# A gated-scan plus ternary-FFN layer on eight cores: layer-norm output transposed on TensorE instead of by DMA, absolute sums moved from VectorE to ScalarE

## The chip, the cores and the metric

The kernel runs on all 8 cores of one Trainium2 chip. Every core executes the same program on its own two sequences (4096 tokens of 2048 channels); the cores exchange nothing. The metric is the device time in microseconds of the slowest core.

## What is computed

The reference, cut to what matters. Every core holds x as [4096, 2048], T=2048 tokens in a sequence, C=2048, H=5120.

```python
x = x + layernorm(attn(layernorm(x), W, b))
x = x + layernorm(ffn(layernorm(x), w_fc, w_proj))

def attn(x, W, b):                       # W: [2C, C]
    gates, values = split(x @ W.T + b)
    gates, values = sigmoid(gates), tanh(values)
    return scan(h[t] = gates[t] * h[t-1] + values[t])

def ternarize(w):
    abs_mean = max(mean(abs(w)), 1e-5)
    thr = 0.7 * abs_mean                 # +1 / -1 / 0, times abs_mean
...
def ffn(x, w_fc, w_proj):
    h = square(relu(x @ ternarize(w_fc).T))
    return h @ ternarize(w_proj).T
```

## The kernel before

The program is a sequence of three stages, each with its own buffers; the five engines (TensorE, VectorE, ScalarE, GpSimd, SyncE) run instruction lists of their own that meet in semaphores.

*Stage 1* (lines 194 to 448) is the one the change touches. GpSimd first casts W to bf16 in HBM and SyncE loads it transposed (`wt_sb`, lines 223 to 226). Then the tokens are worked off in 16 chunks k of 256 tokens (NCH=16, CH1=256). For one chunk: SyncE loads x (`x_sb`, line 234, one buffer); VectorE takes mean and variance (`stats_seg`, lines 46 to 268); ScalarE takes the square root (line 366) and writes the normalised bf16 rows `xnb_sb` (line 371, `ln1_seg`); ScalarE stores them to HBM (`xn_s`, line 377), and SyncE reads them back with 16 transposing DMAs into `xnT_sb` (line 239, three buffers), channels on partitions. TensorE multiplies 32 output groups of 128 channels, a gate group and a value group for each of the 16 channel pairs, each group 16 matmuls of 128x256 (line 418), into four PSUM buffers `ps_par`. ScalarE takes sigmoid and tanh out of PSUM (`evac_seg`, lines 388 and 394), VectorE runs the scan along the tokens for each pair (`scan_seg`, line 285) and keeps its last column in `carry` (line 291). GpSimd stores the 16 pairs of the chunk at once (`h_t`, line 448). `h_sb` has one buffer: the first scan of a chunk waits until the store of the chunk before has landed.

Beside that, stage 1 sums the absolute values of both FFN weight matrices, which gives the two thresholds. The matrices are cut into 320 pieces of 128x512 f32, 20 for each chunk (`wave(k)`). GpSimd loads them into `wslab`, a ring of four buffers (line 445; piece ip waits until piece ip-4 has been summed, semaphore `v_abs`), and VectorE reduces each (`abs_seg`, line 301).

The order of work is written out by hand. On VectorE it is stats of chunk k, scans of chunk k-1, the 20 absolute sums of wave k, then stats of k+1. On ScalarE it is `ln1_seg(k)`, then the 32 evacuations of chunk k-1. On GpSimd it is the 20 loads of wave k, then a wait for all scans of chunk k, then the store of `h_t`. TensorE runs ahead of ScalarE by up to four groups, the depth of `ps_par`:

```python
_w(tensor, s_ev4, gi - 3)      # group gi waits for the evacuation of gi-4
```

After the last chunk VectorE and TensorE exchange a few tiny operations that turn the sums into thresholds (lines 321 to 355, semaphore `fz`).

*Stage 2* (from line 503) reads `h_t` back, transposes it on TensorE (line 573), adds the layer norm of the scan to x, and makes and transposes the ternary weights (lines 583, 551). Its first load, `htin_sb`, waits for every `h_t` store. *Stage 3* (from line 748) is the FFN: matmuls at lines 921 and 933, the long TensorE-bound part. Neither is changed.

Of the kernel before, what the change touches and what calls it, by code (L numbers as in the profile page):

```python
# [53 lines left out]
def build_program(cfg):  # L54
# [47 lines left out]
    with est:  # L102
# [25 lines left out]
        d_xnT4 = ring("d_xnT4", 3); p_mm4 = sem("p_mm4"); s_ev4 = sem("s_ev4")  # L128
        v_sc4 = sem("v_sc4"); v_cr4 = sem("v_cr4"); d_hw4 = ring("d_hw4")
# [48 lines left out]
        with nc.Block() as block:  # L178
# [17 lines left out]
            with contextlib.ExitStack() as sp1:  # L196
# [4 lines left out]
                xnT_sb = sb1("xnT_sb", [128, 3, NC, CH1], BF16)  # L201
# [11 lines left out]
                acc_pj = sb1("acc_pj", [128, NPJP], F32)  # L213
                ps_par = [sp1.enter_context(nc.psum_tensor(f"ps_par{i}", [128, 512], F32))
                          for i in range(4)]
                ps_misc = sp1.enter_context(nc.psum_tensor("ps_misc", [128, 512], F32))
                GP1 = 2 * NG

# [11 lines left out]
                @block.sync  # L230
                def _(sync):
                    for k in range(NCH):
                        _w(sync, s_nm4, TT1 * k)
                        rinc(sync.dma_start(out=x_sb[:, 0, :, :],
                                       in_=x_ch1[k]), d_x4, k)
                        rwait(sync, d_xnw4, k)
                        _w(sync, p_mm4, GP1 * (k - 2))
                        for ct in range(NC):
                            sync.dma_start(
                                out=xnT_sb[:, k % 3, ct, :],  # L240
                                in_=xn_d[k * CH1:(k + 1) * CH1, ct * 128:(ct + 1) * 128],
                                transpose=True).then_inc(d_xnT4[k % 3], 16)
# [3 lines left out]
                def _(vector):  # L246
# [28 lines left out]
                    def scan_seg(vector, k):  # L275
                        for pair in range(NG):
                            gp = k * NG + pair
                            vector.wait_ge(s_ev4, k * GP1 + 2 * pair + 2)
                            rwait(vector, d_hw4, k - 1)
                            if k % RESET == 0:  # L280
                                init = 0.0
                            else:
                                vector.wait_ge(v_cr4, (k - 1) * NG + pair + 1)
                                init = carry[:, pair:pair + 1]
                            vector.tensor_tensor_scan(  # L285
                                out=h_sb[:, 0, pair, :],
                                data0=g_sb[:, gp % 2, :], data1=v_sb[:, gp % 2, :],
                                initial=init, op0=ALU.mult,
                                op1=ALU.add).then_inc(v_sc4, 1)
# [5 lines left out]
                    def abs_seg(vector, k):  # L295
                        for ip in wave(k):
                            rwait(vector, d_wf, ip)
                            kind, a, b, w = pieces[ip]
                            dst = (acc_fc[:, ip:ip + 1] if kind == "fc"
                                   else acc_pj[:, ip - NFCP:ip - NFCP + 1])  # L300
                            vector.tensor_reduce(
                                out=dst, in_=wslab[:, ip % 4, 0:w], axis=AX.X,
                                op=ALU.add, apply_absolute_value=True).then_inc(v_abs, 1)
# [57 lines left out]
                def _(scalar):  # L361
                    scalar.wait_ge(d_prep, 48)

                    def ln1_seg(scalar, k):
# [4 lines left out]
                        rwait(scalar, d_xnw4, k - 1)  # L369
                        for tt in range(TT1):  # L370
# [30 lines left out]
                    for k in range(1, NCH):  # L401
                        ln1_seg(scalar, k)
                        evac_seg(scalar, k - 1)
                    evac_seg(scalar, NCH - 1)

                @block.tensor
                def _(tensor):
                    tensor.wait_ge(d_wt3, 32 * NC)
                    for k in range(NCH):
                        tensor.wait_ge(d_xnT4[k % 3], 16 * NC * (k // 3 + 1))  # L410
                        for pair in range(NG):
                            for role in range(2):
# [4 lines left out]
                                for ct in range(NC):  # L417
# [3 lines left out]
                                        xnT_sb[:, k % 3, ct, :],  # L421
# [550 lines left out]
```

## Time and profile before

| | us |
|---|---|
| five timed runs | 6057.26, 6140.46, 5746.21, 5724.54, 6313.94 |
| their median | 6057.26 |
| the profiled execution | 5741.26 |
| its span, slowest core (core 1) | 5739.7 |
| spans of the other cores | 5702.9 to 5739.6 |

Stage 1 fills the span from its start to about 1907 us, stage 2 to about 2900 us, stage 3 the rest. Times within the trace are microseconds from the start of the span of core 1. In rows of a timeline the first number is the start, the second the time that the row covers; x4 means four instructions merged; the brackets give the idle time of the engine before the row and what ended it.

### The profile page before, as it was taken

What the parts mean: (1) busy time and instruction counts of PE and PEld (TensorE: products, weight loads), DVE (VectorE), ACT (ScalarE), POOL (GpSimd) and SP (SyncE); (2) the same over time, 40 slices, a digit from 0 to 9 for tenths busy, and PEclk for the clock granted to TensorE, in tenths of its full rate; (3) what the DMA queues carried; (4) which work ended last, traced back from release to release, by engine and by line L of the source; (5) the groups of instructions that cost most, each with busy time, mean ns of one, the idle gap of its engine ahead of it and who ended that gap; (6) DMA issues with size and microseconds to landing.
All of it is one profiled execution on the core that took longest, in us unless ns stands there. A gap on an engine that the chain in (4) does not pass through costs nothing.

```text
span 5739.7 us, 60974 instructions; the slowest of 8 cores (5702.9 to 5739.7 us)
## 1 busy us (share of the span) xinstructions
PE 3700.8 (64%) x20742; PEld 2163.6 (38%) x20742; DVE 1492.1 (26%) x2686; ACT 1227.9 (21%) x2768; POOL 246.5 (4%) x460
## 2 busy tenths in 40 slices
PE   0056647466465444443439799596996969879697
PEld 0045536455464322222214344243443434434343
DVE  0022333333333366666610200202002020020101
ACT  0012222121221223232322030220302213031120
POOL 0000110101101000000000000000000000000000
PEclk9977878778787655555569899798997979989898
DMA  9843333433333577776576574655646556474553
GB/s 110 173 114 103 115 115 102 132 104 114 116 101 118 176 245 249 249 243 237 191 185 154 168 174 157 184 156 177 169 143 190 153 189 155 149 191 154 161 151 135
DMA packets 1007452, 918.51 MB, mean 160 GB/s; under 512 B 887216, under 2 KB 887344, under 8 KB 956976
## 3 DMA queue, kind: packets, MB, share of 16 engines
q1 hardware_dynamic: 900528, 486.74, 30.7%
q0 software_dynamic: 47232, 276.85, 16.5%
q10 hardware_dynamic: 59392, 151.02, 8.3%
q8 instruction: 176, 2.88, 0.2%
q14 instruction: 124, 1.02, 0.1%
HBM read 704.76 MB, written 192.94 MB: 156 GB/s over the span
## 4 chain that ended last, share of the span: by engine, by line
PE 58%; DMA 13%; DVE 10%; issue 6%; ACT 5%; SPq 3%; another core or an unknown queue 3%; ACTq 1%; DVEq 0%; POOL 0%; POOLq 0%
PE ps_pj L933 19%; PE ps_fc L921 19%; PE ps_par L418 14%; DMA x_sb<-x 4%; DMA wslab<-wpj 3%; DMA wslab<-wfc 3%; PE ps_bf L583 3%; DVE st6c L46 2%; PE ps_yT L944 2%; DMA sfc_sb<-sfcT_t 2%; ACT stage_fc L551 1%; ACT stage_pj L551 1%; DVE st6a L46 1%; DVE out_sb L811 1%
## 5 line engine op out<-in xcount | busy, mean ns | idle before, releaser
L418 PE MATMUL ps_par<-xnT_sb,wt_sb 128*128 128x256 bf16 x8192 | 948.1, 281 | 957.4 <-ACT g_sb L388 656.0
L921 PE MATMUL ps_fc<-xn1T_sb,sfc_sb 128*128 128x512 bf16 x5120 | 1134.8, 385 | 290.0 <-DMA sfc_sb<-sfcT_t 248.2
L418 PEld LDWEIGHTS ps_par<-xnT_sb,wt_sb 128*128 128x128 bf16 x8192 | 825.5, 101 | 1079.7 <-issue 961.5
L933 PE MATMUL ps_pj<-hfc_sb,spj_sb 128*128 128x512 bf16 x5120 | 1106.5, 379 | 15.6 <-ACT hfc_sb L852 15.6
L921 PEld LDWEIGHTS ps_fc<-xn1T_sb,sfc_sb 128*128 128x128 bf16 x5120 | 506.4, 99 | 916.6 <-issue 331.7
L933 PEld LDWEIGHTS ps_pj<-hfc_sb,spj_sb 128*128 128x128 bf16 x5120 | 500.3, 98 | 621.7 <-issue 19.9
L46 DVE BATCH_NORM_STATS2 st6c<-ps_yT 128x6 f32<-128x512 f32 x128 | 79.7, 684 | 2367.2 <-PE ps_yT L944 2367.2
L583 PE MATMUL ps_bf<-idbf_sb,ssl 128*128 128x128 bf16 x1280 | 295.8, 265 | 357.3 <-DVE ssl L657 160.2
L848 ACT ACTIVATE r_sb<-ps_fc,am_fc 128x512 f32<-128x512 f32 x320 | 220.0, 687 | 686.8 <-PE ps_fc L921 682.8
L583 PEld LDWEIGHTS ps_bf<-idbf_sb,ssl 128*128 128x128 bf16 x1280 | 134.2, 105 | 521.7 <-issue 484.8
L285 DVE TENSOR_TENSOR_SCAN h_sb<-g_sb,carry,v_sb 128x256 f32<-128x256 f32 x224 | 168.1, 750 | 602.5 <-ACT v_sb L394 593.2
L860 ACT COPY y_sb<-ps_pj 128x512 f32<-128x512 f32 x128 | 75.0, 586 | 1039.6 <-PE ps_pj L933 1039.6
L573 PE MATMUL ps_hT<-id_sb,htin_sb 128*128 128x128 f32 x512 | 115.2, 419 | 193.7 <-DVE x1o_sb L629 180.8
L944 PE MATMUL ps_yT<-id_sb,y_sb 128*128 128x128 f32 x512 | 100.8, 380 | 207.2 <-DVE out_sb L811 207.2
L852 ACT ACTIVATE hfc_sb<-r_sb 128x512 bf16<-128x512 f32 x320 | 201.3, 629 | 30.0 <-ACT r_sb L848 0.7
L366 ACT ACT_TABLE_LOAD x15 | 19.2, 1283 | 853.7 <-DVE veps L257 853.7
L388 ACT ACTIVATE g_sb<-ps_par,bT_sb 128x256 f32<-128x256 f32 x256 | 121.4, 474 | 343.4 <-PE ps_par L418 312.5
L394 ACT ACTIVATE v_sb<-ps_par,bT_sb 128x256 f32<-128x256 f32 x256 | 121.5, 475 | 299.2 <-PE ps_par L418 299.2
L551 ACT COPY stage_fc<-ps_bf 128x128 bf16<-128x128 bf16 x640 | 146.0, 266 | 178.2 <-PE ps_bf L583 160.5
L551 ACT COPY stage_pj<-ps_bf 128x128 bf16<-128x128 bf16 x640 | 151.8, 266 | 144.9 <-PE ps_bf L583 121.9
L573 PEld LDWEIGHTS ps_hT<-id_sb,htin_sb 128*128 128x128 f32 x512 | 104.3, 226 | 201.1 <-issue 199.2
L944 PEld LDWEIGHTS ps_yT<-id_sb,y_sb 128*128 128x128 f32 x512 | 92.0, 201 | 216.2 <-issue 214.5
(75 smaller groups left out, 1676.6 us busy)
## 6 DMA issues: line engine op xcount, KB each, us to landing
sfc_sb<-sfcT_t SPq DMA_DIRECT2D x320, 512.0 KB, 4.9
spj_sb<-spjT_t SPq DMA_DIRECT2D x128, 1280.0 KB, 6.2
wslab<-wfc POOLq DMA_DIRECT2D x160, 256.0 KB, 4.2
wslab<-wpj POOLq DMA_DIRECT2D x160, 256.0 KB, 3.6
wslab<-wfc ACTq DMA_DIRECT2D x160, 256.0 KB, 4.9
wslab<-wpj ACTq DMA_DIRECT2D x160, 256.0 KB, 4.0
x_sb<-x SPq DMA_DIRECT2D x16, 2048.0 KB, 8.5
h_t<-h_sb POOLq DMA_DIRECT2D x16, 2048.0 KB, 9.5
```

What stands on the lines that cost most here:

```text
L46: ins = vec.bn_stats(st6[:, 6 * j:6 * j + 6], src[:, j * step:(j + 1) * step])
L285: vector.tensor_tensor_scan(out=h_sb[:, 0, pair, :], data0=g_sb[:, gp % 2, :], data1=v_sb[:, gp % 2, :], initial=init, op0=ALU.mult, op1=A ...
L394: scalar.activation(out=v_sb[:, gp % 2, :], in_=ps_par[gi % 4][:, 0:CH1], func=AF.Tanh, bias=bT_sb[:, NG + pair:NG + pair + 1]).then_inc(s ...
L418: ins = tensor.matmul(pp[:, 0:CH1], wt_sb[:, ct, col0:col0 + 128], xnT_sb[:, k % 3, ct, :], start=(ct == 0), stop=(ct == NC - 1))
L551: scalar.copy(out=dst, in_=ps_bf[t % 2][0:128, 0:128]).then_inc(s_ev2, 1)
L573: tensor.transpose(ps_hT[hf][:, ctl * 128:(ctl + 1) * 128], htin_sb[:, k % 2, ct, tt * 128:(tt + 1) * 128], id32[:, :]).then_inc(p_tr7, 1)
L583: tensor.transpose(ps_bf[t % 2][0:128, 0:128], ssl2[:, ip % 2, ctl * 128:(ctl + 1) * 128], idbf[:, :]).then_inc(p_tr2, 1)
L848: scalar.activation(out=r_sb[:, 0, :], in_=ps_fc[gh % 2][:, 0:CH2], func=AF.Relu, scale=am_fc[:, 0:1]).then_inc(s_rev, 1)
L852: scalar.activation(out=hfc_sb[:, ht, :], in_=r_sb[:, 0, :], func=AF.Square).then_inc(s_sqq, 1)
L921: ins = tensor.matmul(ps_fc[gh % 2][:, 0:CH2], sfc_sb[:, gh % 3, ct, :], xn1T_sb[:, q % 2, ct, :], start=(ct == 0), stop=(ct == NC - 1))
L933: ins = tensor.matmul(ps_pj[gc % 2][:, 0:CH2], spj_sb[:, gc % 2, ht, :], hfc_sb[:, ht, :], start=(ht == 0), stop=(ht == NH - 1))
L944: tensor.transpose(ps_yT[:, ct * 128:(ct + 1) * 128], y_sb[:, ct, tt * 128:(tt + 1) * 128], id32[:, :]).then_inc(p_yt, 1)
```

## The change

The layer-norm output no longer goes through HBM. After ScalarE has written `xnb_sb`, TensorE transposes it in 128x128 blocks into two new PSUM tiles `ps_xt` (`xt_group`, four groups of eight blocks for a chunk), and VectorE copies each block into `xnT_sb` (`xevac_one`, eight copies for a group). `xnT_sb` now has two buffers. The groups for chunk k+1 are placed on TensorE behind matmul groups 7, 15, 23 and 31 of chunk k, and on VectorE ahead of the scans of pairs 2, 6, 10 and 14 of chunk k. Those for chunk 0 stand ahead of everything.

The absolute sums go from VectorE to ScalarE: `abs_seg` becomes an activation with the function Abs and an accumulator output, its elementwise result going to a scratch tile `absdump`. It stands behind the evacuations of its own chunk; each piece also waits for the one before it. GpSimd's list is not changed.

```diff
@@ sync @@
                         rinc(sync.dma_start(out=x_sb[:, 0, :, :],
                                        in_=x_ch1[k]), d_x4, k)
-                        rwait(sync, d_xnw4, k)
-                        _w(sync, p_mm4, GP1 * (k - 2))
-                        for ct in range(NC):
-                            sync.dma_start(
-                                out=xnT_sb[:, k % 3, ct, :],
...
@@ vector @@
-                    def scan_seg(vector, k):
+                    def scan_seg(vector, k, xk=None):
                         for pair in range(NG):
+                            if xk is not None and pair % max(1, NG // NXG) == 2 % max(1, NG // NXG):
+                                g = pair // max(1, NG // NXG)
+                                if g < NXG:
+                                    xevac_one(vector, xk, g)
...
+                    def xevac_one(vector, k, g):
+                        tt, co = g // 2, (g % 2) * TPG
+                        vector.wait_ge(p_xt, TPC * k + TPG * (g + 1))
+                        for ci in range(TPG):
+                            ins = vector.tensor_copy(
+                                out=xnT_sb[:, k % 2, co + ci,
+                                           tt * 128:(tt + 1) * 128],
+                                in_=ps_xt[g % 2][0:128, ci * 128:(ci + 1) * 128])
+                        ins.then_inc(v_xe, 1)
 
                     vcnt = stats_seg(vector, 0, vcnt)
-                    abs_seg(vector, 0)
+                    for g in range(NXG):
+                        xevac_one(vector, 0, g)
                     for k in range(1, NCH):
                         vcnt = stats_seg(vector, k, vcnt)
-                        scan_seg(vector, k - 1)
-                        abs_seg(vector, k)
+                        scan_seg(vector, k - 1, xk=k)
                     scan_seg(vector, NCH - 1)
@@ scalar @@
-                        rwait(scalar, d_xnw4, k - 1)
+                        _w(scalar, p_xt, NC * TT1 * k)
...
-                        scalar.wait_ge(s_nm4, TT1 * (k + 1))
-                        rinc(scalar.dma_start(out=xn_ch1[k],
-                                         in_=xnb_sb[:, 0, :, :]), d_xnw4, k)
+
+                    def abs_seg(scalar, k):
+                        for ip in wave(k):
+                            rwait(scalar, d_wf, ip)
+                            _w(scalar, v_abs, ip)
+                            kind, a, b, w = pieces[ip]
+                            dst = (acc_fc[:, ip:ip + 1] if kind == "fc"
+                                   else acc_pj[:, ip - NFCP:ip - NFCP + 1])
+                            scalar.activation(
+                                out=absdump[:, 0:w], in_=wslab[:, ip % 4, 0:w],
+                                func=AF.Abs, accum_out=dst).then_inc(v_abs, 1)
...
                     for k in range(1, NCH):
                         ln1_seg(scalar, k)
                         evac_seg(scalar, k - 1)
+                        abs_seg(scalar, k - 1)
                     evac_seg(scalar, NCH - 1)
+                    abs_seg(scalar, NCH - 1)
@@ tensor @@
+                    def xt_group(tensor, k, g):
+                        tt, co = g // 2, (g % 2) * (NC // 2)
+                        tensor.wait_ge(s_nm4, TT1 * (k + 1))
+                        _w(tensor, v_xe, NXG * k + g - 1)
+                        for ci in range(NC // 2):
+                            tensor.transpose(
+                                ps_xt[g % 2][0:128, ci * 128:(ci + 1) * 128],
+                                xnb_sb[:, 0, tt, (co + ci) * 128:(co + ci + 1) * 128],
+                                idbf[:, :]).then_inc(p_xt, 1)
...
                     for k in range(NCH):
-                        tensor.wait_ge(d_xnT4[k % 3], 16 * NC * (k // 3 + 1))
+                        tensor.wait_ge(v_xe, NXG * (k + 1))
...
+                                gidx = 2 * pair + role
+                                per = GP1 // NXG
+                                if k + 1 < NCH and (gidx + 1) % per == 0:
+                                    g = gidx // per
+                                    if g < NXG:
+                                        xt_group(tensor, k + 1, g)
```

The order on ScalarE from the last evacuations of chunk 0 (`v_sb`, `g_sb`) to the first of chunk 1, before the change:

```order
L388 ACTIVATE g_sb<-ps_par,bT_sb 128x256
L394 ACTIVATE v_sb<-ps_par,bT_sb 128x256
L366 ACTIVATE sd<-veps 128x2
L371 ACTIVATE xnb_sb<-x_sb,nmrs,rs 128x2048 x2
L377 DMA xn_s<-xnb_sb 128x2x2048
L388 ACTIVATE g_sb<-ps_par,bT_sb 128x256
```

The same place on ScalarE with the change:

```order
L401 ACTIVATE g_sb<-ps_par,bT_sb 128x256
L407 ACTIVATE v_sb<-ps_par,bT_sb 128x256
L389 ACTIVATE absdump,acc_fc<-wslab 128x512 x20
L371 ACTIVATE sd<-veps 128x2
L376 ACTIVATE xnb_sb<-x_sb,nmrs,rs 128x2048 x2
L401 ACTIVATE g_sb<-ps_par,bT_sb 128x256
```

The 20 absolute sums now stand between the evacuations of one chunk and the normalisation that precedes the next, and the store of `xn_s` is gone.

TensorE at the end of a quarter of a chunk with the change (the list before has the 8192 matmuls of line 418 in a row, without anything between):

```order
L428 MATMUL ps_xt<-idbf_sb,xnb_sb 128x128 x8
L445 MATMUL ps_par<-xnT_sb,wt_sb 128x256 x128
L428 MATMUL ps_xt<-idbf_sb,xnb_sb 128x128 x8
L445 MATMUL ps_par<-xnT_sb,wt_sb 128x256 x128
L428 MATMUL ps_xt<-idbf_sb,xnb_sb 128x128 x8
```

Eight transposes follow every eight groups (128 matmuls).

VectorE within chunk 1's scans with the change (the list before has only the scan and carry rows):

```order
L287 SCALAR_TENSOR_TENSOR h_sb<-g_sb,carry,v_sb 128x256
L293 COPY carry<-h_sb 128x1
L304 COPY xnT_sb<-ps_xt 128x128 x8
L287 SCALAR_TENSOR_TENSOR h_sb<-g_sb,carry,v_sb 128x256
L293 COPY carry<-h_sb 128x1
```

Eight copies stand ahead of every fourth scan. The scan itself is the first row's instruction in both lists.

SyncE around the first x load before the change:

```order
L234 DMA x_sb<-x 128x2x2048
L239 DMA_TRANSPOSE xnT_sb<-xn_s 128x256 [waits d_xnw40]
L239 DMA_TRANSPOSE xnT_sb<-xn_s 128x256 x15
L234 DMA x_sb<-x 128x2x2048 [waits s_nm4]
```

And with the change:

```order
L231 DMA_TRANSPOSE wt_sb<-wbf_s 128x2048
L235 UNCONDITIONAL_BRANCH
L239 DMA x_sb<-x 128x2x2048
L239 DMA x_sb<-x 128x2x2048 [waits s_nm4] x15
L530 UNCONDITIONAL_BRANCH
```

Each x load now follows the one before it directly and waits only for `s_nm4`, the end of the normalisation that read `x_sb`.

## Rows read from the trace of the kernel before

**Rows 1.** Busy time by stretch, core 1 (engines, granted TensorE clock, DMA share, GB/s)
```profile
600.00:1000.00 400.00, 223.19 (x1970) 196.03 (x1969) 132.29 (x263) 84.45 (x143) 44.89 (x84) 0.78 0.36 116
3300.00:5740.00 2440.00, 2046.34 (x9400) 960.47 (x9397) 270.13 (x484) 490.48 (x744) 24.17 (x46) 0.92 0.57 164
```
**Rows 2.** Timeline, TensorE, stage 1
```profile
301.40 9.11 PE L418 MATMUL ps_par<-xnT_sb,wt_sb 128*128 128x256 bf16 x64 [301.40 <-DMA xnT_sb<-xn_s]
323.81 69.38 PE L418 MATMUL ps_par<-xnT_sb,wt_sb 128*128 128x256 bf16 x512 [13.30 <-ACT g_sb L388]
440.66 62.52 PE L418 MATMUL ps_par<-xnT_sb,wt_sb 128*128 128x256 bf16 x512 [47.47 <-ACT g_sb L388]
547.52 57.71 PE L418 MATMUL ps_par<-xnT_sb,wt_sb 128*128 128x256 bf16 x512 [44.34 <-ACT g_sb L388]
...
1774.45 65.60 PE L418 MATMUL ps_par<-xnT_sb,wt_sb 128*128 128x256 bf16 x576 [43.07 <-ACT g_sb L388]
```
**Rows 3.** Timeline, all engines, one turn of stage 1
```profile
750.98 0.47 ACT L388 ACTIVATE g_sb<-ps_par,bT_sb 128x256 f32<-128x256 f32 x1
...
802.82 0.47 ACT L394 ACTIVATE v_sb<-ps_par,bT_sb 128x256 f32<-128x256 f32 x1 [1.27 <-PE ps_par L418]
...
804.84 0.54 POOL L448 DMA_DIRECT2D h_t<-h_sb  x1 [72.55 <-DVE h_sb L285]
...
815.01 2.78 DVE L301 TENSOR_REDUCE acc_fc<-wslab 128x1 f32<-128x512 f32 x4 [10.47 <-DMA wslab<-wfc]
...
839.95 2.46 DVE L46 BATCH_NORM_STATS2 st6a<-x_sb 128x6 f32<-128x512 f32 x4
...
845.93 1.28 ACT L366 ACT_TABLE_LOAD   x1 [42.64 <-DVE veps L257]
...
854.22 0.47 ACT L388 ACTIVATE g_sb<-ps_par,bT_sb 128x256 f32<-128x256 f32 x1
```
**Rows 4.** Instructions of line 301 (min/median/max ns)
```profile
L301 DVE TENSOR_REDUCE acc_fc<-wslab x160: 675/686/687, 269.7 to 1043.5; 128x1 f32<-128x512 f32 x160
```
**Rows 5.** Groups of instructions, ScalarE, whole span
```profile
L852 ACT ACTIVATE hfc_sb<-r_sb 128x512 bf16<-128x512 f32 x320 | 201.3, 629 | 30.0 <-ACT r_sb L848 0.7
L551 ACT COPY stage_pj<-ps_bf 128x128 bf16<-128x128 bf16 x640 | 151.8, 266 | 144.9 <-PE ps_bf L583 121.9 <-DVE nbs L652 19.9 <-issue 0.5
```
**Rows 6.** The page, costliest groups: the bf16 transposes of stage 2
```profile
L583 PE MATMUL ps_bf<-idbf_sb,ssl 128*128 128x128 bf16 x1280 | 295.8, 265 | 357.3 <-DVE ssl L657 160.2
```
**Rows 7.** The page, DMA issues: KB each, median us from issue to landing
```profile
h_t<-h_sb POOLq DMA_DIRECT2D x16, 2048.0 KB, 9.5
```
**Rows 8.** Timeline, the start of stage 1
```profile
269.91 4.08 ACT L371 ACTIVATE xnb_sb<-x_sb,nmrs,rs 128x2048 bf16<-128x2048 f32 x2 [0.70 <-DVE nmrs L268]
...
300.08 0.51 SPq L234 DMA_DIRECT2D x_sb<-x  x1
...
310.24 2.47 DVE L46 BATCH_NORM_STATS2 st6a<-x_sb 128x6 f32<-128x512 f32 x4 [11.15 <-DMA x_sb<-x]
...
323.19 0.47 ACT L388 ACTIVATE g_sb<-ps_par,bT_sb 128x256 f32<-128x256 f32 x1
```
**Rows 9.** Timeline, the last two chunks and the start of stage 2
```profile
1833.22 0.47 ACT L394 ACTIVATE v_sb<-ps_par,bT_sb 128x256 f32<-128x256 f32 x1 [1.27 <-PE ps_par L418]
...
1905.63 0.47 ACT L394 ACTIVATE v_sb<-ps_par,bT_sb 128x256 f32<-128x256 f32 x1 [1.27 <-PE ps_par L418]
...
1907.65 0.54 POOL L448 DMA_DIRECT2D h_t<-h_sb  x1 [50.60 <-DVE h_sb L285]
...
1925.11 3.65 PE L573 MATMUL ps_hT<-id_sb,htin_sb 128*128 128x128 f32 x16 [12.87 <-DMA htin_sb<-h_t]
```
**Rows 10.** Busy time by stretch, core 1: TensorE clock in chunk 0, and later
```profile
340.00:360.00 20.00, 20.00 (x155) 16.58 (x153) 3.53 (x9) 4.53 (x10) 0.00 (x0) 0.81 0.38 126
760.00:802.00 42.00, 42.00 (x387) 37.64 (x386) 10.86 (x24) 11.39 (x24) 0.00 (x0) 1.00 0.22 69
3700.00:3900.00 200.00, 198.08 (x919) 89.68 (x917) 0.00 (x0) 47.55 (x74) 0.00 (x0) 1.00 0.56 155
```

More of the change, by code:

```diff
@@ L128, in build_program @@
         d_xnT4 = ring("d_xnT4", 3); p_mm4 = sem("p_mm4"); s_ev4 = sem("s_ev4")
+        p_xt = sem("p_xt"); v_xe = sem("v_xe")
         v_sc4 = sem("v_sc4"); v_cr4 = sem("v_cr4"); d_hw4 = ring("d_hw4")
@@ L200, in build_program @@
                 xnb_sb = sb1("xnb_sb", [128, 1, TT1, C], BF16)
-                xnT_sb = sb1("xnT_sb", [128, 3, NC, CH1], BF16)
+                xnT_sb = sb1("xnT_sb", [128, 2, NC, CH1], BF16)
                 g_sb = sb1("g_sb", [128, 2, CH1], F32)
@@ L213, in build_program @@
                 acc_pj = sb1("acc_pj", [128, NPJP], F32)
+                absdump = sb1("absdump", [128, max(PW, PWP)], F32)
                 ps_par = [sp1.enter_context(nc.psum_tensor(f"ps_par{i}", [128, 512], F32))
@@ L216, in build_program @@
                 ps_misc = sp1.enter_context(nc.psum_tensor("ps_misc", [128, 512], F32))
+                ps_xt = [sp1.enter_context(nc.psum_tensor(f"ps_xt{i}", [128, 1024], BF16))
+                         for i in range(2)]
                 GP1 = 2 * NG
+                NXG = 2 * TT1
                 @block.sync
@@ L235, in _ @@
                                        in_=x_ch1[k]), d_x4, k)
-                        rwait(sync, d_xnw4, k)
-                        _w(sync, p_mm4, GP1 * (k - 2))
-                        for ct in range(NC):
-                            sync.dma_start(
-                                out=xnT_sb[:, k % 3, ct, :],
-                                in_=xn_d[k * CH1:(k + 1) * CH1, ct * 128:(ct + 1) * 128],
-                                transpose=True).then_inc(d_xnT4[k % 3], 16)
                 @block.vector
@@ L293, in scan_seg @@
                                 in_=h_sb[:, 0, pair, CH1 - 1:CH1]).then_inc(v_cr4, 1)
[L295 to L303, printed above, removed]
+                    TPG = NC // 2
+                    TPC = NC * TT1
+                    def xevac_one(vector, k, g):
[7 more added lines that the diff above has]
+                        ins.then_inc(v_xe, 1)
                     vcnt = stats_seg(vector, 0, vcnt)
-                    abs_seg(vector, 0)
+                    for g in range(NXG):
+                        xevac_one(vector, 0, g)
                     for k in range(1, NCH):
                         vcnt = stats_seg(vector, k, vcnt)
-                        scan_seg(vector, k - 1)
-                        abs_seg(vector, k)
+                        scan_seg(vector, k - 1, xk=k)
                     scan_seg(vector, NCH - 1)
@@ L403, in _ @@
                         evac_seg(scalar, k - 1)
+                        abs_seg(scalar, k - 1)
                     evac_seg(scalar, NCH - 1)
+                    abs_seg(scalar, NCH - 1)
                 @block.tensor
                 def _(tensor):
+                    def xt_group(tensor, k, g):
[7 more added lines that the diff above has]
+                                idbf[:, :]).then_inc(p_xt, 1)
                     tensor.wait_ge(d_wt3, 32 * NC)
+                    for g in range(NXG):
+                        xt_group(tensor, 0, g)
                     for k in range(NCH):
-                        tensor.wait_ge(d_xnT4[k % 3], 16 * NC * (k // 3 + 1))
+                        tensor.wait_ge(v_xe, NXG * (k + 1))
                         for pair in range(NG):
@@ L420, in _ @@
                                         wt_sb[:, ct, col0:col0 + 128],
-                                        xnT_sb[:, k % 3, ct, :],
+                                        xnT_sb[:, k % 2, ct, :],
                                         start=(ct == 0), stop=(ct == NC - 1))
                                 ins.then_inc(p_mm4, 1)
+                                gidx = 2 * pair + role
[4 more added lines that the diff above has]
+                                        xt_group(tensor, k + 1, g)
                     tensor.wait_ge(d_prep, 48)
```

## The prediction

> **What bounds the kernel now.** I read the busy time by stretch first. In stage 3 TensorE works for 2046 of 2440 us, in stage 1 for only 223 of 400, and no other engine fills the rest: VectorE has 132 us, ScalarE 84 [rows 1]. So stage 1 is a chain that goes round between engines. TensorE's timeline shows its period: bursts of 512 matmuls in 57.7 us, with 43 to 47 us of nothing between them, ended each time by ScalarE emptying a PSUM buffer [rows 2]. From 547.52 to 1774.45 are 12 turns, 102.2 us each. The timeline of all engines then shows one turn [rows 3]. From the first evacuation (750.98) to the end of the last (802.82 + 0.47) are 52.3 us, paced by TensorE. The 50.9 us until the next evacuation (854.22) are serial:
> - 11.7 us to the first absolute sum (815.01): the last scan, then the store of h_t, behind which GpSimd issues the first four weight pieces;
> - 24.9 us for the 20 sums and the gaps between them (to 839.95);
> - 6.0 us of statistics (to 845.93);
> - 8.3 us: table load, square root, normalisation, table load (to 854.22).
>
> TensorE is ready all that time, four groups ahead. Its idle time is bought by VectorE's absolute sums and by the weight ring behind the store.
>
> **The change, part by part.**
>
> *Removed from the turn.* With the sums off VectorE, the statistics of the next chunk run right behind the last scan, while ScalarE sums. x is there: its load no longer stands behind 16 transposes on SyncE, only behind the normalisation. So 11.7 us and 6.0 us leave the path. The first four pieces are in the ring long before, because GpSimd issued them after the last store, a whole evacuation phase earlier.
>
> *The sums on ScalarE.* VectorE needs 686 ns for a piece [rows 4], and 20 of them took 24.9 us, so 11 us are landings that the four-deep ring does not hide; these stay. ScalarE's nearest row, a 512-wide activation from SBUF, is 629 ns [rows 5]; the accumulator output and the wait for the previous piece come on top, and neither is shown by a row. Bounds: 24 us, if ScalarE is no slower (its activation is 57 ns shorter), and 30 us, if each piece takes 1.5 us of engine time, over twice the row. I take 25.7, near the low end, because the ring and not the engine paces the rows. Behind them queue the square root and the normalisation, and they are then the path: 8.3 us, less some 0.2 for the DMA issue that goes. One turn without evacuations becomes 25.7 + 8.3 = 34.0 us in place of 50.9: 16.9 saved.
>
> *Transposes on TensorE.* Three of the four groups of eight fall inside the evacuation phase; the fourth follows the last matmul group. A matmul of 256 columns goes by every 109 ns (52.3 us for 28 groups with the slow start; 42 us for 387 [rows 10]). Eight blocks of half the columns would be 0.44 us; at stage 2's latency of 265 ns for each [rows 6] 2.1 us. I take 0.5: stage 2's 265 ns belong to transposes that wait for their buffers, these eight are issued in a row. 3 x 0.5 = 1.5 us for a turn, bounds 1.3 to 6.4.
>
> *Copies on VectorE.* Eight copies stand ahead of the scans of pairs 2, 6, 10 and 14, and wait there for groups 7, 15, 23 and 31. The nearest copy is ScalarE's from PSUM, 266 ns [rows 5]; eight are 2.1 us. While VectorE waits and copies, TensorE works through the four free buffers. The evacuation of group 8 needs the scan of pair 2, and TensorE needs that buffer only for group 12, four groups or 7 us after the transposes; copies, scan and evacuation take 2.1 + 0.8 + 0.5. About 3.5 us are spare, so I cost this at nothing. At 4 us and more for eight copies it would cost. The statistics behind the last copies have 25.7 us of cover.
>
> *The store of h_t.* It is issued when the last weight load has gone out, some 4 us before the sums end, and lands 9.5 us later [rows 7], near 5.5 us after that end. The first scan of the next chunk comes at 8.3 + 0.8 us. Covered; above 12.5 us it would be late. Such a delay is again first taken up by the four buffers.
>
> *The sum.* (a) Start: the second x load was issued at 300.08, behind the transposes of chunk 0, and the first evacuation came at 323.19 [rows 8]. Now it is issued when the first normalisation ends, at 274.0: 26 us earlier. Transposes and copies of chunk 0, about 10 us for four groups, lie beside that load. I take -25. (b) From the evacuation of chunk 0 to that of chunk 14 are 14 turns: 14 x (1.5 - 16.9) = -215.6. (c) Chunk 15: before, VectorE did the sums while TensorE was ahead; from the end of chunk 14's evacuation to that of chunk 15's were 1906.10 - 1833.69 = 72.4 us [rows 9]. Now 25.7 + 52.3 = 78.0, and 1.5 for chunk 14's transposes: +7.1. (d) End: the sums of chunk 15 now come last. The store of h_t was issued 1.5 us after the last evacuation, stage 2 began 17.5 us later [rows 9]; now it is issued after 25.7 - 4 = 21.7 us: +20. The threshold operations fit beside the 17.5 us as before. Together -25 - 215.6 + 7.1 + 20 = -213.5 us. Stages 2 and 3 are untouched. Against the profiled execution's 5741.3 that is 5528 us, -3.7%.
>
> The median of the five runs shown, 6057.3, is 5.5% above that execution, and the lowest of them is 5724.5. The same cut in an execution like the median gives 5528 x 1.055 = 5832. The point is made for the profiled kind, the range reaches the other.
>
> **Where the Trainium skill speaks.** Rows first: 686 ns on VectorE and 629 ns on ScalarE for 512 f32 columns [rows 4, 5]. "ScalarE: Activation LUTs", rules for kernel authors, speaks against the move: cheap functions belong on VectorE, which it puts up to three times faster, but for bf16. By that rule the sums would lengthen; in f32 the rows show no such difference, so the trace does not bear it out here. The same page's section on table sets says that abs is in every set; if so, no third table load comes in. No run here shows it yet.
>
> **Rivals.**
>
> *The clock falls in stage 1.* In chunk 0 this core's granted clock was 0.81 of 2.4 GHz with TensorE always busy, in the later ones 1.00 [rows 10], and that burst took 69.4 us, not 57.7 [rows 2]. With shorter pauses more cores multiply at once. 14 turns at +11.7 are +164: 5692, -0.9%. Against it: in stage 3, with 198 of 200 us busy, the clock was 1.00 [rows 10]. "TensorE: Matmul & The Clock Gate", Part 1, tells of a current limiter at 13/16 once three cores of a die run dense matmuls; chunk 0 agrees in size, stage 3 does not.
>
> *The store or the copies hold the scans.* If h_t lands 10 us later than I think, or the eight copies take 5.5 us (686 ns each, as the slow VectorE row), TensorE stalls 5 to 9 us a turn: +75 to +135, about 5630, -1.9%. For it: GpSimd's store is now queued behind three weight loads. Against: it was queued ahead of four before, and the bus is freer without the transposes.
>
> *Slower: the ring becomes serial on ScalarE.* If the accumulating activation frees its buffer late (a drain for each piece, the wait on the previous one, GpSimd waking again), only two loads are in flight. Four buffers at 24.9 / 20 = 1.25 us a piece make a round trip of 5.0 us (sum, wake, issue, landing). Half of it for each piece is 2.5 us, 50 us for 20, +24.3 in each of 16 waves: +389, 5917, +3.1%. It decides from the point where a piece costs 2.3 us: 213.5 + 115 us over 320 pieces is 1.03 on top of 1.28. Against it: 686 and 629 ns are alike, and VectorE's ring held 1.25 us a piece.
>
> *An extra table load* at each wave, 1.28 us as in [rows 3], is +20 and inside the forecast's own range.
>
> **How the numbers follow.** Forecast 0.80, at 5528; its own range 5480 (shorter landings, a better clock at the start) to 5640 (30 us for the sums and slow transposes would be 5673, both together unlikely). Clock 0.07, store or copies 0.09, serial ring 0.04. About 2% (115 us) is what a measurement of this kernel can tell from no change. Faster by more: the forecast and part of the third case, 0.85. Within 2%: 0.11. Slower by more: 0.04. The range, 5460 to 5840, takes in the clock and store cases, and at its top an execution like the median's.
>
> **What would show it.** Right: turns of about 87 us between bursts on TensorE; gaps of some 25 us, not 44; statistics on VectorE beside the sums; the 20 sums in 24 to 27 us; stage 2 beginning near 1710 us instead of 1925. Wrong: sums of 40 us or more; VectorE's scans released by the h_t store; TensorE waiting inside a burst; a granted clock of 0.81 in bursts after chunk 1.

## The result, and the profile after

The changed kernel is faster. The ratio to the kernel before is 0.9593, with a 95% interval of 0.9553 to 0.9632: 4.1% less. All timed runs together have a median of 5736.82 us (6 runs, 5504.72 to 6090.12) against 6024.02 us (10 runs) before. Both kernels have executions in which the cores of a die show a lower clock and the time is longer; the ratios leave those out, the medians do not.

| us | before | after | difference |
|---|---|---|---|
| profiled execution | 5741.26 | 5504.93 | -236.3 |
| span of the slowest core | 5739.7 (core 1) | 5503.3 (core 6) | -236.4 |
| first evacuation, chunk 0 | 323.2 | 293.0 | -30.2 |
| 14 turns, chunk 0 to chunk 14 | 1450.6 | 1230.0 | -220.6 |
| from there to the first matmul of stage 2 | 151.3 | 175.3 | +24.0 |
| from there to the end | 3814.6 | 3805.0 | -9.6 |

The timeline of TensorE in the changed kernel answers to [rows 2]. A chunk now shows as several rows, since the transposes of line 428 stand between the matmuls; the rows below are those that follow a wait.

```profile
278.22 8.80 PE L445 MATMUL ps_par<-xnT_sb,wt_sb 128*128 128x256 bf16 x64 [1.60 <-DVE xnT_sb L304]
...
561.50 8.81 PE L445 MATMUL ps_par<-xnT_sb,wt_sb 128*128 128x256 bf16 x64 [27.58 <-ACT g_sb L401]
615.52 7.15 PE L445 MATMUL ps_par<-xnT_sb,wt_sb 128*128 128x256 bf16 x64 [1.50 <-DVE xnT_sb L304]
650.86 8.51 PE L445 MATMUL ps_par<-xnT_sb,wt_sb 128*128 128x256 bf16 x64 [28.19 <-ACT g_sb L401]
704.57 7.15 PE L445 MATMUL ps_par<-xnT_sb,wt_sb 128*128 128x256 bf16 x64 [1.50 <-DVE xnT_sb L304]
```

The idle time between bursts is 28 us where it was 44 us, and the releaser is the same as before: ScalarE's first evacuation. A second, new wait of 1.50 us stands at each chunk's first matmul, for VectorE's last copies. It costs nothing, since TensorE then only fills its four PSUM buffers and stops until ScalarE comes back (704.57 to 711.72, then nothing until 741.12).

The timeline of all engines over one turn answers to [rows 3].

```profile
650.24 0.47 ACT L401 ACTIVATE g_sb<-ps_par,bT_sb 128x256 f32<-128x256 f32 x1
...
659.20 0.61 PE L428 MATMUL ps_xt<-idbf_sb,xnb_sb 128*128 128x128 bf16 x8
...
659.92 1.14 DVE L304 COPY xnT_sb<-ps_xt 128x128 bf16<-128x128 bf16 x8 [6.50 <-PE ps_xt L428]
...
702.78 0.47 ACT L407 ACTIVATE v_sb<-ps_par,bT_sb 128x256 f32<-128x256 f32 x1 [1.27 <-PE ps_par L445]
703.15 0.62 ACT L389 ACTIVATE absdump<-wslab 128x512 f32<-128x512 f32 x1
...
703.67 0.19 ACT L389 ACTIVATION_READ_ACCUMULATOR absdump<-wslab 128x1 f32 x1
703.95 0.63 ACT L389 ACTIVATE absdump<-wslab 128x512 f32<-128x512 f32 x1
...
706.28 2.47 DVE L46 BATCH_NORM_STATS2 st6a<-x_sb 128x6 f32<-128x512 f32 x4
...
725.59 0.54 POOL L481 DMA_DIRECT2D h_t<-h_sb  x1
729.26 0.63 ACT L389 ACTIVATE absdump<-wslab 128x512 f32<-128x512 f32 x1 [4.76 <-DMA wslab<-wfc]
...
732.44 1.28 ACT L371 ACT_TABLE_LOAD   x1
```

ScalarE begins the sums in the same microsecond in which it ends the evacuations: four pieces lie ready. VectorE takes the statistics from 706.28 on, beside the sums, and has them long before ScalarE asks at 732.44. The phase from 650.24 to 703.25 is 53.0 us, the wave from 703.15 to the table load 29.3 us, the rest to the next evacuation (740.5) 8.1 us. The store of h_t is issued at 725.59, behind the loads of the last four pieces (722.47 to 725.06), and ScalarE waits 4.76 us for the first of these four. The rows do not show that the store is the reason: in the next wave ScalarE waits 4.6 and 4.0 us before the store is issued.

The instructions of line 389 and what they waited for answer to [rows 4].

```profile
L389 ACT ACTIVATE absdump<-wslab x320: 618/629/633, 347.0 to 1677.2; 128x512 f32<-128x512 f32 x160
L389 ACT ACTIVATION_READ_ACCUMULATOR absdump<-wslab x320: 184/186/193, 347.5 to 1677.7; 128x1 f32 x160
its engine sat idle before it (us, times) until:
  DMA wslab<-wfc: 103.7, 68
  DMA wslab<-wpj: 71.2, 84
```

The accumulator output is a second instruction of 186 ns. With it a piece takes 0.81 us of the engine when the next lies ready (703.15 to 703.95), against 0.69 on VectorE, and 175 us of waiting for landings, over all 16 waves, come on top. The chip's clock in the bursts answers to [rows 10]: busy time by stretch, columns as there.

```profile
300.00:340.00 40.00, 40.00 (x381) 35.96 (x379) 12.29 (x46) 10.66 (x23) 0.00 (x0) 1.00 0.01 1
561.50:565.00 3.50, 3.50 (x17) 2.44 (x18) 1.81 (x4) 0.95 (x3) 0.00 (x0) 0.51 0.96 379
615.52:622.60 7.08, 7.08 (x64) 6.16 (x64) 6.58 (x14) 4.24 (x13) 3.12 (x7) 1.00 0.55 174
664.00:700.00 36.00, 36.00 (x340) 32.34 (x339) 11.14 (x36) 9.46 (x20) 0.00 (x0) 1.00 0.01 2
3000.00:4000.00 1000.00, 831.88 (x3811) 390.26 (x3810) 123.94 (x228) 213.09 (x319) 12.58 (x24) 0.91 0.60 169
```

Behind a pause of 27.6 us a burst has a mean clock of 0.51 in its first 3.5 us, the 1.2 GHz level, and 1.00 after them, the 2.4 GHz level; behind a pause of 1.5 us it is at 1.00 from its first matmul.

### The profile page after: what moved, and what is told of

Same layout as the page of the kernel before. It is cut to its first block, busy times and chain, and to the rows that moved or that the text cites. A ratio compares the mean times of both kernels' runs of the same rounds, so it can differ in the third digit from the quotient of the medians.

```text
span 5503.3 us, 63022 instructions; the slowest of 8 cores (5442.7 to 5503.3 us)
## 1 busy us (share of the span) xinstructions
PE 3715.3 (68%) x21254; PEld 2183.7 (40%) x21254; DVE 1344.0 (24%) x2878; ACT 1450.9 (26%) x3408; POOL 246.9 (4%) x460
## 4 chain that ended last, share of the span: by engine, by line
PE 61%; DMA 11%; DVE 8%; ACT 7%; issue 6%; another core or an unknown queue 3%; SPq 2%; ACTq 1%; POOL 0%; DVEq 0%; POOLq 0%
PE ps_pj L966 20%; PE ps_fc L954 19%; PE ps_par L445 15%; DMA x_sb<-x 4%; PE ps_bf L616 3%; DMA wslab<-wfc 3%; DVE st6c L46 2%; DMA wslab<-wpj 2%; PE ps_yT L977 2%; ACT stage_fc L584 1%; ACT stage_pj L584 1%; DVE out_sb L844 1%; DMA x1a_sb<-x_s 1%; PE ps_hT L606 1%
## 5 line engine op out<-in xcount | busy, mean ns | idle before, releaser
L445 PEld LDWEIGHTS ps_par<-xnT_sb,wt_sb 128*128 128x128 bf16 x8192 | 813.3, 100 | 530.9 <-issue 421.1
L389 ACT ACTIVATE absdump<-wslab 128x512 f32<-128x512 f32 x320 | 201.2, 629 | 189.1 <-DMA wslab<-wfc 103.7
L428 PE MATMUL ps_xt<-idbf_sb,xnb_sb 128*128 128x128 bf16 x512 | 40.5, 225 | 272.7 <-ACT xnb_sb L376 272.2
```

The costliest lines, as they stand in the source:

```text
L389: scalar.activation(out=absdump[:, 0:w], in_=wslab[:, ip % 4, 0:w], func=AF.Abs, accum_out=dst).then_inc(v_abs, 1)
L445: ins = tensor.matmul(pp[:, 0:CH1], wt_sb[:, ct, col0:col0 + 128], xnT_sb[:, k % 2, ct, :], start=(ct == 0), stop=(ct == NC - 1))
```

## The experiments

Theory: a turn is the evacuation phase plus what stands in a row behind it. The change is worth what it takes out of that row (the statistics and the wait for the first weight piece), and that depends on where the sums stand, not on which engine makes them. The transposes on TensorE are worth the start alone. Rivals: the DMA transposes took bandwidth from the weight pieces; or VectorE's load was the bound. For each kernel I give the time of the profiled execution and, from its timeline, the turn: first evacuation of chunk 0 to that of chunk 14, over 14. A wave is the time from the first to the last sum of a chunk, as a mean of 16. A phase is the time from the first to the last evacuation of a chunk, and the gap is what lies between two phases.

| kernel | time, us | turn | wave |
|---|---|---|---|
| before | 5741.3 | 103.6 | 24.2 |
| changed | 5504.9 | 87.9 | 26.2 |
| e1, sums on ScalarE only | 5528.6 | 86.9 | 26.0 |
| e2, transposes on TensorE only | 5783.2 | 105.3 | 23.8 |
| e3, changed, seven weight buffers | 5403.0 | 80.2 | 18.5 |
| e6, before, sums between the scans | 5250.9 | 68.8 | - |
| e4, changed, sums between the evacuations | 5236.9 | 70.5 | - |
| e7, e6 with early statistics | 5124.0 | 61.5 | - |
| e5, e4 with early statistics | 5105.0 | 62.5 | - |
| e8, changed again | 5714.6 | 87.8 | 26.0 |

### e1: the sums alone

```diff
# in the kernel before
-                        abs_seg(vector, k)
...
                         evac_seg(scalar, k - 1)
+                        abs_seg(scalar, k - 1)
...
-                xnT_sb = sb1("xnT_sb", [128, 3, NC, CH1], BF16)
+                xnT_sb = sb1("xnT_sb", [128, 2, NC, CH1], BF16)
```

> Only the absolute sums move to ScalarE, behind the evacuations; the transposes stay DMAs (with two xnT buffers instead of three, since the scratch tile needs the room). My theory: the turn is the serial part between evacuation phases plus the phase itself, and only the sums' place shortens it. Turn = 87.9 us of the changed kernel less 1.8 for the three transpose groups, about 86; the start stays at 323 (first evacuation), 30 us later than with the change. 5505 + 30 - 14 x 1.8 = about 5510, the same as the changed kernel within 10 us. Rival: the DMA transposes and the trip through HBM cost bandwidth that the weight pieces need; then the 20 sums stay longer than the 26.4 us mean of the changed kernel, turns are 90 us or more, and the time is 5560 or more.

Measured: 5528.6, ratio 0.962 (0.960 to 0.9641), turn 86.9, wave 26.0. The DMA transposes take nothing from the weight pieces: the wave is as long with them as without. Of the changed kernel's gain in the turns, all is here and a microsecond more, for the transposes that TensorE need not make (mean phase 52.4 us against 53.7). The time is 19 us above the 5510 expected: the first evacuation came at 331.7 and not at 323, because the first statistics of this execution ended 11 us later than in the kernel before.

### e2: the transposes alone

```diff
# in the changed kernel
                         scan_seg(vector, k - 1, xk=k)
+                        abs_seg(vector, k)
...
-                        abs_seg(scalar, k - 1)
```

> Only the transposes move to TensorE; the absolute sums stay on VectorE behind the scans. My theory: the DMA transposes were hidden behind the matmuls, so this gains only the start (30 us) and pays three transpose groups of 0.6 us and some copies in each of 15 turns (about 2 to 3 us a turn, 30 to 45 us): 5725 to 5760, no change within 1%. Rival: relieving the DMA queues shortens the wait for the weight pieces (10.5 us for the first, 24 us for the twenty) by several us a turn: 5680 or less.

Measured: 5783.2, without an interval; turn 105.3, wave 23.8. It is 23 us above my range: I had credited it with the start of 30 us, and it has almost none. The first evacuation came at 328.8; counted from the end of the first statistics that is 50.2 us, where the kernel before took 55.6 and the changed one 27.3. In this kernel VectorE sums wave 0 before the statistics of chunk 1, as before the change; the early x load is of no use without the sums' move. So even the start needs both parts. The timeline shows why the turn does not shorten (all engines, from the last transposes of a chunk to the normalisation):

```profile
704.30 0.54 POOL L479 DMA_DIRECT2D h_t<-h_sb  x1 [74.24 <-DVE h_sb L286]
704.83 2.12 POOL L476 DMA_DIRECT2D wslab<-wfc  x4
715.71 2.67 DVE L302 TENSOR_REDUCE acc_fc<-wslab 128x1 f32<-128x512 f32 x4 [11.70 <-DMA wslab<-wfc]
...
738.85 2.46 DVE L46 BATCH_NORM_STATS2 st6a<-x_sb 128x6 f32<-128x512 f32 x4
...
744.84 1.28 ACT L382 ACT_TABLE_LOAD   x1 [43.91 <-DVE veps L254]
```

The store, then the landing that VectorE waits 11.7 us for, the sums and the statistics stand in one row, as in [rows 3].

### e3: seven weight buffers

```diff
# in the changed kernel, lines 212, 390, 476, 478; the ring of semaphores d_wf grows to seven too
-                wslab = sb1("wslab", [128, 4, max(PW, PWP)], F32)
+                wslab = sb1("wslab", [128, 7, max(PW, PWP)], F32)
...
-                            _w(gpsimd, v_abs, ip - 3)
+                            _w(gpsimd, v_abs, ip - 6)
```

> The changed kernel with seven wslab buffers instead of four (GpSimd waits for piece ip-7). Theory one: the 26.4 us for 20 sums are the round trip of a buffer (issue, landing, sum) over four buffers; with seven the engine paces, 0.82 us a piece, 16.4 to 18 us for 20, 8 to 10 us less in each of 16 waves: 5345 to 5375. Theory two: the pieces come at the rate that the DMA engines give in that stretch (about 210 GB/s, 1.25 us a piece of 256 KB); then only the three more resident pieces gain, about 3.5 us a wave: about 5450.

Measured: 5403.0, ratio 0.9405 (0.9385 to 0.9425), turn 80.2, wave 18.5. Between the two expectations, and nearer to theory one: the wave fell by 7.7 us to within 2.1 us of the engine's 16.4 (20 pieces at 0.82), where theory two allowed 3.5. ScalarE's rows of one wave:

```profile
691.26 0.63 ACT L389 ACTIVATE absdump<-wslab 128x512 f32<-128x512 f32 x1
...
692.08 0.63 ACT L389 ACTIVATE absdump<-wslab 128x512 f32<-128x512 f32 x1
...
694.22 0.63 ACT L389 ACTIVATE absdump<-wslab 128x512 f32<-128x512 f32 x1 [1.42 <-DMA wslab<-wfc]
...
696.32 0.63 ACT L389 ACTIVATE absdump<-wslab 128x512 f32<-128x512 f32 x1 [1.38 <-DMA wslab<-wfc]
```

The seven pieces that lie ready go by at 0.82 us; a few landings of 1.4 us are left. So the round trip of a buffer paced the wave, as the prediction said. The time is 28 us above my 5375, and half of that is the start: the first statistics ended at 281.2 in that execution and not at 265.6, and the first evacuation was at 307.6 and not at 293.0.

### e6: before, with the sums between the scans

```diff
# in the kernel before
     def scan_seg(vector, k):
         for pair in range(NG):
...
+            abs_n(vector, k * PPC + (pair * PPC) // NG,
+                  k * PPC + ((pair + 1) * PPC) // NG)
...
-                        abs_seg(vector, k)
```

> The kernel before with DMA transposes and the sums on VectorE as before, but one or two sums behind each scan of chunk k instead of twenty behind the last (wave k goes with chunk k). Theory place: what the change gained came from where the sums stand, not from the engine; VectorE has 2.5 us idle in each 3.5 us pair, the sums need 0.86. Then between the last evacuation and the next there are 1.1 us scan, 6 us statistics and 8.3 us normalisation: turns of 68 to 70 us instead of 103.6, 72 to 55 us for the last chunk: about 5240 to 5260, far below the changed kernel. Theory engine: VectorE's load is the bound and taking work off it is what helped; then the evacuation phase grows by the sums (20 x 0.69 = 13.7 us or more), turns are 85 or more and the time is above 5480.

Measured: 5250.9, ratio 0.9128 (0.9111 to 0.9144), turn 68.8. Nothing changed engine, and the gain is twice that of the change (8.7% against 4.1%). The timeline shows how the sums fit (all engines, one pair, and the end of the chunk):

```profile
714.83 0.75 DVE L295 TENSOR_TENSOR_SCAN h_sb<-g_sb,carry,v_sb 128x256 f32<-128x256 f32 x1 [1.85 <-ACT v_sb L394]
715.69 0.15 DVE L301 COPY carry<-h_sb 128x1 f32<-128x1 f32 x1
715.79 0.69 DVE L281 TENSOR_REDUCE acc_fc<-wslab 128x1 f32<-128x512 f32 x1
...
733.60 0.54 POOL L448 DMA_DIRECT2D h_t<-h_sb  x1 [7.87 <-DVE h_sb L295]
...
734.45 2.46 DVE L46 BATCH_NORM_STATS2 st6a<-x_sb 128x6 f32<-128x512 f32 x4
...
740.44 1.28 ACT L366 ACT_TABLE_LOAD   x1 [8.38 <-DVE veps L257]
```

VectorE still waits 1.85 us in a pair, for ScalarE's next evacuation. ScalarE's wait for the variance, 42.6 us in [rows 3], is 8.4 us. The theory of VectorE's load falls: in the kernel before VectorE was idle and badly ordered. Wave k now goes beside chunk k, so that chunk 15 too has sums in its phase, which is 54.6 us and not 78.1.

### e4: the changed kernel, sums between the evacuations

```diff
# in the changed kernel, evac_seg
+                                g = 2 * pair + role
+                                lo, hi = (g * PPC) // GP1, ((g + 1) * PPC) // GP1
+                                for j in range(lo, hi):
+                                    if k * PPC + j < NPIECE:
+                                        abs_one(scalar, k * PPC + j)
...
-                        abs_seg(scalar, k - 1)
```

> The changed kernel with the 20 sums of a wave spread behind the evacuations on ScalarE (0 or 1 behind each of the 32) instead of in a row behind the last. ScalarE has 1.27 us idle after each evacuation, a sum with its accumulator read takes 0.82. Theory place: the 26 us of the wave disappear from the turn; what remains between the evacuation phases is the tail of the scans (3 us, behind the last transposes and copies), 6 us of statistics and 8.3 us: turns of 71 us instead of 87.9, about 5220. Rival: the sums do not fit into the gaps of 1.27 us (the wait on a landing piece holds the evacuation behind it, TensorE runs out of PSUM buffers), the evacuation phase grows from 53.6 to 60 us or more, and the time is 5320 or more.

Measured: 5236.9, without an interval; turn 70.5, phases of 53.0 to 54.8 us, 61.0 in the last chunk. Against the 5741.3 of the kernel before, measured on another occasion, it is 8.8% less. The sums fit into the gaps and the rival falls. The profile of ScalarE at the end of a chunk:

```profile
700.16 0.47 ACT L406 ACTIVATE v_sb<-ps_par,bT_sb 128x256 f32<-128x256 f32 x1 [0.66 <-PE ps_par L447]
700.53 0.62 ACT L388 ACTIVATE absdump<-wslab 128x512 f32<-128x512 f32 x1
701.05 0.19 ACT L388 ACTIVATION_READ_ACCUMULATOR absdump<-wslab 128x1 f32 x1
709.66 1.28 ACT L371 ACT_TABLE_LOAD   x1 [8.42 <-DVE veps L255]
```

What is late next is VectorE's statistics, 8.42 us.

### e5 and e7: the statistics between the scans too

```diff
# e5, in e4; e7 has the same in e6, ahead of pairs 12 and 14
     for pair in range(NG):
+        if sk is not None and pair == 8:
+            bn_tt(vector, sk, 0)
+        if sk is not None and pair == 12:
+            bn_tt(vector, sk, 1)
+            veps_seg(vector, sk)
```

> e4 with the statistics of the next x chunk between the scans (ahead of pairs 8 and 12), so that only the square root, the normalisation and two table loads stand between the evacuation phases. Expected: turns of 63 to 64 us, about 5115. Rival: TensorE becomes the bound (59.7 us of work a chunk and a wait for the last copies) or its granted clock falls to 0.81 in the bursts because more cores multiply at once; then turns are 70 or more, 5200 or more.

> e6 (DMA transposes, sums on VectorE between the scans, turn 68.8) with the same early statistics (ahead of pairs 12 and 14). Nothing of the change under study is in it. If the transposes on TensorE are worth nothing once the order is right, this has turns of 61 to 62 us and ends at 5130 to 5150, within 0.5% of e5. If the DMA transposes collide with the x load and the weight pieces, the statistics wait for x and the turn stays at 66 or more: 5210 or more.

Measured: e5 5105.0, ratio 0.8559 (0.8487 to 0.8631), turn 62.5; e7 5124.0, turn 61.5. Both come out at or just below what was expected. e7 has nothing of the change in it; it is 0.4% above e5 in total and 1 us a turn below it: in the best order, too, the whole change gives only an earlier start (first evacuation 292.8 against 324.4) and costs about a microsecond in each turn. The two kernels differ in the engine of the sums as well as in the transposes, so that microsecond is put down to the transposes by its size alone (after less e1 is 1.0 us too). e5's ratio says more than it should: its own cores had a mean granted clock of 0.857, the two executions of the kernel before that it is set against (5954 and 5977 us) one of 0.775 to 0.797. Against the kernel before's 5741.3, measured on another occasion, e5 is 11.1% less, and against the changed kernel's 5504.9 it is 7.3% less. In e5 a turn's serial part is 9.1 us. Its rows (ScalarE, VectorE):

```profile
729.85 0.20 ACT L388 ACTIVATE sd<-veps 128x2 f32<-128x2 f32 x1
730.00 0.75 DVE L295 TENSOR_TENSOR_SCAN h_sb<-g_sb,carry,v_sb 128x256 f32<-128x256 f32 x1
...
731.67 4.08 ACT L393 ACTIVATE xnb_sb<-x_sb,nmrs,rs 128x2048 bf16<-128x2048 f32 x2 [1.62 <-DVE nmrs L270]
735.77 1.28 ACT L417 ACT_TABLE_LOAD   x1
...
739.41 0.75 DVE L295 TENSOR_TENSOR_SCAN h_sb<-g_sb,carry,v_sb 128x256 f32<-128x256 f32 x1 [7.89 <-DMA h_t<-h_sb]
```

Here the store of h_t is what the first scan of each of the chunks 1 to 15 waits for, 124.7 us in all; in the changed kernel that happened once, in the last chunk. TensorE's buffers take most of it up: it sits idle for under 4 us a turn, so that it is now near to being the bound itself. The clock rival had its hardest test here, with TensorE busy 376 of 400 us:

```profile
600.00:1000.00 400.00, 376.18 (x3519) 334.46 (x3518) 156.13 (x509) 220.80 (x500) 73.50 (x137) 1.00 0.47 160
```

### e8: the changed kernel again

> The changed kernel once more, unchanged, beside the others, since the time at which stage 1 starts differed by up to 15 us between runs (first statistics done at 267 us in one profile, at 280 in others). Expected: 5505 to 5520, ratio 0.957 to 0.963; turn 87 to 88 us.

Measured: 5714.6, ratio 0.9581 (0.95 to 0.9661), turn 87.8. The time is off by 200 us and the ratio is not. On core 0, the slowest, stage 1 is the same as in the first profile: its turn, and the first matmul of stage 2 at 1702.9 against 1698.3. Its loss is in stage 3, where its granted clock was lower. The second row is core 2 of the same execution, in a burst of stage 1:

```profile
3000.00:4000.00 1000.00, 831.47 (x3202) 366.92 (x3264) 124.03 (x228) 191.12 (x285) 12.63 (x24) 0.78 0.54 151
700.00:740.00 40.00, 40.00 (x319) 33.42 (x317) 11.15 (x42) 8.54 (x18) 0.00 (x0) 0.81 0.00 1
```

The same 831 us of busy time hold 3202 recorded matmuls at 0.78, where the first profile has 3811 at 0.91. Core 2, in turn, had 0.91 in that stretch of stage 3, but 0.81 in its bursts of stage 1, and so had core 3 in nearly all of its own: their turns are 97.0 and 94.8 us, where the same cores took 87.7 and 86.0 in the first profile. Cores 0 and 1 of the same die had 1.00 in their bursts and turns of 87.8 and 85.6. The chip as such was not slower on this occasion, since e4, e5 and e7 ran beside e8 with 0.91 to 0.93 on every core in the same stretch of stage 3. The ratio comes out right because the executions of the kernel before beside it had a lower clock too (0.775 to 0.797, e8's cores 0.794 to 0.808). A time, or a ratio, may be read only with the granted clock of both executions beside it.

## Why the prediction was right and where it was wrong

*The mechanism was right, term by term.*
- Gap between evacuation phases: 34.0 us predicted, 34.2 measured (mean of 14). The wave was put at 25.7 and took 26.2; before, the gap was 50.2 in the mean, a little less than the 50.9 of the one turn that I had read.
- Phase: +1.5 us predicted for three transpose groups, +1.3 measured: the mean phase is 53.7 us, that of chunks 2 to 13 before was 52.4. The row of a group covers 0.61 us, but the next matmul begins 0.45 us after its start (570.15 to 570.60), near the 0.44 that I had as the lower bound.
- 14 turns: -215.6 predicted, -220.6 measured. That this is so close is in part luck, since two misses cancel. A gap gave back 16.0 us and not 16.9, which is 12.3 us less over 14 turns. The 14 phases grew by 3.7 us in all and not by 21: chunks 0 and 1 took 62.2 and 56.8 us before, beginning at a granted clock of 0.81 that cores 0 and 1 alone had there [rows 10], and 54.1 and 53.2 in the changed kernel, where no core had it. Those 11.7 us are not the change's doing.
- Last chunk and end: +7.1 + 20 predicted, +24.0 measured.
- Start: -25 predicted, -30.2 measured. The second x load was issued at 272.1, 28 us earlier than before; 2 us of these are an earlier first normalisation in that execution. It landed 8.5 us after issue and not 10.2. e2 adds what I had missed: the start needs the sums' move as well.
- Stages 2 and 3: 0 predicted, -9.6 measured. From the first matmul of stage 2 to the end the same code took 3798.7 to 3821.4 us in the profiles of before, after and e1 to e7, so this is spread.

The sum is -236.4 where -213.5 was forecast: right in sign and within 11%.

*The step that failed is what the sum was set against.* "Against the profiled execution's 5741.3 that is 5528 us, -3.7%", with "The point is made for the profiled kind, the range reaches the other". The paragraph of that second sentence gave the median of the runs shown, 6057.3, 5.5% above that execution. A point of 5528 beside that median reads as -8.7%, more than twice the 4.1% that was measured; and the median of the timed runs came out at 5736.8, not 5528. The point forecast should have stood on the same footing as the number it would be read against: 6057.3 - 213.5, or x 0.963, is 5833 to 5844, the value that I had myself worked out as 5832 and used only as an upper end. The measured medians, 6024.0 and 5736.8, differ by 4.8%. Measured against the profiled execution alone the point is 0.4% off.

*The rivals.* The clock did not fall in the changed kernel's profile: 1.00 in the bursts behind their first 3.5 us, and in e5 at 94% busy. In e8, the same kernel, it did: 0.81 on cores 2 and 3 in nearly every burst of stage 1, and on cores 4 and 5 in some late ones. It cost cores 2 and 3 about 9 us a turn, near the 11.7 that the rival gave it. The kernel before had the same level on two cores in its chunks 0 and 1, so nothing shows that the change brings it about; how often either kernel meets it is open. "TensorE: Matmul & The Clock Gate" of the Trainium skill, Part 1, tells of a limiter at 13/16 when three cores of a die run dense matmuls; the bursts of the first profile do not show it, though their pauses are shorter. e8's rows agree with it in size (0.81), but do not tell a cause, and cores 0 and 1 of the same die had 1.00 in their bursts. The copies, predicted at 2.1 us, took 1.14 and did not hold TensorE, which has no pause inside a burst; ScalarE's first evacuation behind a group waits 1.82 us where 1.27 is usual. (The prediction's own numbers put the point from which the copies cost at 2.1 + 3.5 = 5.6 us, not at 4.) The store held a scan once, the first of the last chunk (released at 1604.31), and there TensorE went on without a pause. The ring did not become serial. No third table load came in: lines 371 and 401 have 15 table loads each in stage 1, as lines 366 and 388 had, and line 389 has none, which bears out "ScalarE: Activation LUTs" of the Trainium skill, section on table sets. The same page's rule in its section for kernel authors, which puts cheap functions on VectorE, has a point even in f32, 0.81 us against 0.69, but it was not what decided, since landings paced both (e3).

*What the prediction did not see* is how much the order was worth. It named VectorE's sums as what bought TensorE's idle time, and took their engine to be the cure. e6 shows that their place was: without a change of engine it gains 8.7%, where the change gains 4.1%.

## What to carry to other kernels

When a long row of small, independent instructions stands at one point of a turn, look first for the gaps that its own engine has in the same turn; spreading it there (e6) was worth twice what handing it to another engine in one piece was. A transfer that the matmuls already hide gives nothing back when it becomes TensorE and VectorE work (e1, e2); it can only shorten the start. And set the forecast against the number that will be timed: if the profiled execution and the median of the runs differ by more than the effect, say the effect as a ratio and derive the point from both.

## What the runs showed of the hardware

- An activation with an accumulator output is two instructions: 629 ns and a read of 186 ns. A row of them goes by at 0.81 us a piece.
- Eight bf16 transposes of 128x128 in a row cover 0.61 us at a granted clock of 1.00 and hold up the next matmul by 0.45 us, though each is listed at 225 ns in the mean; eight VectorE copies of 128x128 bf16 from PSUM take 1.14 us, each listed at 213 ns. The step from one row's start to the next row's, not the mean of one instruction, prices a series. My 2.1 us for the copies came from a ScalarE row of 266 ns times eight.
- The first 64 matmuls of a burst took 8.5 to 8.8 us behind a pause of 28 us and 7.15 us behind one of 1.5 us, where the granted clock is 1.00 from the start. e5, whose pauses in the later turns are all of 1.7 us or less, has 7.15 at the head of a chunk (729.25 to 736.40), and its phases from chunk 4 on are 52.3 us in the mean and not 53.7.
- A granted clock of 0.81 can stand on some cores of a die and not on others through a whole stage: in e8 cores 2 and 3 had 0.81 and cores 0 and 1 had 1.00 in the bursts of stage 1.
- The waves of the first weight matrix were longer on ScalarE (28.3 us, mean of the first eight) than those of the second (24.0), more than before (25.2 and 23.3 for VectorE). The store of h_t now goes out among the last landings of a wave and not ahead of the first, which holds for both matrices; why the first suffers more was not tried.
